# Counts of edges in windows of 16 nodes instead of 32, one incidence tile on ScalarE, and another order on VectorE and GpSimd

## What is computed

```python
h = maximum(_ln(x), 0)
m = mlp3(concat(h[src], h[dst], edge_attr), mW1, mW2, mW3)      # 32768 x 320 -> 256 -> 256 -> 128
summed = segment_sum(m, src) + segment_sum(m, dst)
x = x + mlp3(concat(h, summed, attention(h)), uW1, uW2, uW3)
h = maximum(_ln(x), 0)
deg = segment_sum(1, dst) + 1                                    # with a loop at every node
xw = h @ W
out = segment_sum(deg[src]**-.5 * deg[dst]**-.5 * xw[src], dst)  # loops included
x = x + gelu(out + b)
```

## Time and profile before

| | us |
|---|---|
| median of three runs | 767.0 |
| profiled execution, its own time | 765.72 |
| its span, first to last instruction | 763.9 |
| PE, DVE, ACT, POOL busy | 736.0, 729.5, 524.3, 539.0 |
| TensorE's mean granted clock | 0.994 |

### The profile page before, as it was taken

One profiled execution on the slowest core, in us unless ns is written; L12 is line 12 of the kernel. 1 busy time (PEld: TensorE's weight loads), 2 busy tenths in 40 slices (PEclk: granted clock), 3 DMA queues, 4 the chain that ended last, 5 costly groups with the idle time before them and its releaser, 6 DMA issues.

```text
span 763.9 us, 13342 instructions
## 1 busy us (share of the span) xinstructions
PE 736.0 (96%) x4171; PEld 619.3 (81%) x4171; DVE 729.5 (96%) x1506; ACT 524.3 (69%) x711; POOL 539.0 (71%) x533
## 2 busy tenths in 40 slices
PE   7589999999999999999999999999999999999896
PEld 6467888888888888888888888888888888888755
DVE  7889999999999999999999999999999999999775
ACT  3256777777777777777777777777777777776623
POOL 3777777777777777777777777777777777777100
PEclk9899999999999999999999999999999999999999
DMA  7534444344434444344443444434443444432000
GB/s 227 164 119 129 128 127 123 117 126 129 126 112 125 130 128 127 114 124 128 127 124 113 130 129 126 126 112 127 129 126 113 126 127 130 126 111 83 0 1 28
DMA packets 42566, 90.15 MB, mean 118 GB/s; under 512 B 11136, under 2 KB 17920, under 8 KB 42496
## 3 DMA queue, kind: packets, MB, share of 16 engines
q0 software_dynamic: 24576, 67.14, 28.6%
q1 hardware_dynamic: 17920, 22.16, 9.9%
HBM read 86.64 MB, written 2.62 MB: 117 GB/s over the span
## 4 chain that ended last, share of the span: by engine, by line
PE 88%; DVE 4%; POOL 3%; issue 2%; DMA 2%; ACT 1%; DVEq 0%; SPq 0%; POOLq 0%
PE bank L628 30%; PE bank L607 22%; PE bank L617 14%; PE bank L587 7%; PE bank L593 7%; PE bank L646 4%; POOL rows_sb L446 2%; POOL rows_sb L454 1%; DVE ring L1005 1%; PE bank L720 1%; DMA w_sb<-mW 1%; PE bank L765 1%; PE bank L728 1%; DMA table_a<-rows_sb 0%; PE bank L714 0%
## 5 line engine op out<-in xcount | busy, mean ns | idle before, releaser
L446 POOL DMA_INDIRECT rows_sb<-table_a,ends_i x256 | 263.5, 1029 | 82.2 <-issue 77.7
L454 POOL DMA_INDIRECT rows_sb<-table_b,ends_i x256 | 262.7, 1026 | 78.0 <-issue 78.0
L812 ACT ACTIVATE dist<-iota_h,neg_mid 128x1026 f16<-128x1026 f16 (+1 forms) x256 | 292.3, 1143 | 0.0
L1005 DVE TENSOR_SCALAR ring<-dist,half_gap,times 128x1026 fp32r<-128x1026 f16 (+1 forms) x256 | 276.4, 1081 | 1.7 <-ACT dist L812 0.6
L628 PE MATMUL bank<-ring,m_hi 128*128 128x512 f32 x512 | 172.4, 418 | 1.3 <-DVE ring L1005 1.1
L802 ACT ACTIVATE h_sb<-bank,b_sb 128x512 f32<-128x512 f32 x128 | 87.6, 684 | 122.5 <-PE bank L607 122.5
L628 PE MATMUL bank<-ring,m_lo 128*128 128x512 f32 x512 | 160.8, 395 | 0.0
L607 PE MATMUL bank<-ring,w_hi 128*128 128x512 f32 x512 | 150.0, 394 | 1.4 <-DVE ring L985 1.4
L1057 DVE TENSOR_SCALAR oh_key<-iota_h,key_f,minus_base 128x258 bf16<-128x258 f16 x321 | 128.5, 400 | 0.0
L617 PE MATMUL bank<-w_sb,h_sb 128*128 128x128 f32 x1024 | 124.8, 275 | 0.0
L593 PE MATMUL bank<-ident,rows_sb 128*128 128x128 f32 x512 | 113.7, 276 | 8.0 <-DVE rows_sb L1048 8.0
(11 more groups left out here) (182 smaller groups left out, 628.5 us busy)
## 6 DMA issues: line engine op xcount, KB each, us to landing
e_raw<-edge_attr_t SPq DMA_DIRECT2D x128, 128.0 KB, 3.1
rows_sb<-table_a,ends_i POOLq DMA_INDIRECT x256, 2.8
rows_sb<-table_b,ends_i POOLq DMA_INDIRECT x256, 2.9
table_a<-rows_sb SPq DMA_DIRECT2D x4, 256.0 KB, 3.4
table_b<-rows_sb SPq DMA_DIRECT2D x4, 256.0 KB, 2.5
x_sb<-x SPq DMA_DIRECT2D x2, 256.0 KB, 3.2
out<-oh_key SPq DMA_DIRECT2D x4, 128.0 KB, 1.8
u_sb<-uW SPq DMA_DIRECT2D x1, 384.0 KB, 5.0
```

Source lines behind the costliest of these rows:

```text
L446: nc.gpsimd.indirect_dma_start(got[:, b, t, 0, :], None, table_a, bass.IndirectOffsetOnAxis(ap=ends_i[:, 0, tile:tile + 1], axis=0),).then ...
L454: nc.gpsimd.indirect_dma_start(got[:, b, t, 1, :], None, table_b, bass.IndirectOffsetOnAxis(ap=ends_i[:, 1, tile:tile + 1], axis=0),).then ...
L812: nc.scalar.activation(to, of, ACT.Abs, bias=neg_mid[:, bass.ds(g * GT + t, 1)]).then_inc(dist_ready, 1)
L1005: nc.vector.tensor_scalar(to, of, half_gap[:, tile], times[:, tile], ALU.is_equal, ALU.mult).then_inc(inc_ready, 1)
```

## The change

The counts are made in 64 windows of 16 nodes, six tiles each, one window a group; `oh_key` is flat with 128 columns. The first six windows are made two at a time in DVE's groups -1, 0 and 1 and counted in PE's groups 0, 1 and 2. A pair of windows goes from PSUM to the counts by an add on DVE. `ct_sb` is cleared and its diagonal set at the start, on ACT, and `more_windows` runs then. Three incidence tiles stay on DVE, now all in rows, and the fourth is made on ACT as relu(times - times * abs(distance - gap)), except in the last group. DVE's list is reordered. In the last group the bias comes before the scatters, and the scatters go half by half. POOL only gathers.

The diff, cut to what matters:

```diff
-    VT = 10
-    NW = 32
+    VT = 6
+    NW = 64
     WD = N // NW
     WK = WD * NC
-    KR, KN, KP = 3, 86, 88
+    PAIRS = NW // 2
+    PD = 2 * WD
+    PK = 2 * WK
     MORE = NW * TILES
...
+    HOT = 4
     PAIR_ATT = 32
     DR, DN, DP = 3, 342, 344
-    IN_ROWS = (0, 2)
+    IN_ROWS = (0, 1, 2)
+    DT = GT - 1
     assert D == P and 2 * ED == P and H == 2 * P and GROUPS % 2 == 0
...
         ct_sb = sb("ct_sb", [P, NC, N])
         into_part = sb("into_part", [P, N])
-        from_part = sb("from_part", [P, NW, NC])
...
         w1_hi, w1_lo = inc[:, 1, 0:2 * H], inc[:, 1, 2 * H:4 * H]
-        iota_f = ct_sb[:, 0, :]
...
-        LAST_W = 2 * (NW - 1)
-
-        def made_in(i):
-
-            return 0 <= i and i + 1 < NW
-
-        def summed_in(b, i):
-
...
+        FILL = 2
+
+        def made_in(g):
+
+            if g < FILL:
+                return [2 * (g + 1), 2 * (g + 1) + 1]
+            return [w for w in (g + 2 + FILL,) if w < NW]
+
+        def counted_in(g):
+
+            if 0 <= g <= FILL:
+                return [2 * g, 2 * g + 1]
+            return [w for w in (g + 1 + FILL,) if FILL < g and w < NW]
+
+        def summed_in(g):
+
+            pairs = [p for p in range(PAIRS) if 2 * p + 1 in counted_in(g - 1)]
+            return pairs[0] if pairs else None
+
+        LAST_SUM = NW - 1 - FILL
...
-            pool.wait_ge(ld_w, 16 * 12)
-            nc.gpsimd.tensor_tensor(xb_sb[:, :, :], x_sb[:, :, :],
-                                    ub3_all[:, :].unsqueeze(1).broadcast_to([P, NC, D]), ALU.add).then_inc(xb_ready, 1)
-
-            pool.wait_ge(into_ready, 1)
-            diagonal = ct_all[:, 0:(NC - 1) * (N + P)].rearrange("p (s n) -> p s n", n=N + P)[:, :, 0:P]
-            nc.gpsimd.tensor_tensor(diagonal, diagonal, ident[:, :].unsqueeze(1).broadcast_to([P, NC - 1, P]), ALU.add)
-            diagonal = ct_all[:, (NC - 1) * (N + P):NC * N]
-            nc.gpsimd.tensor_tensor(diagonal, diagonal, ident[:, :], ALU.add).then_inc(self_added, 1)
-
...
                                           start=False, stop=True, is_transpose=True, skip_group_check=True)
-                    if counting and t in COUNTS_AT[k]:
...
+            def wait_incidence(g, t):
+
+                if t < DT or g == GROUPS - 1:
+                    pe.wait_ge(inc_ready, DT * g + (t + 1))
+                else:
+                    pe.wait_ge(last_inc_ready, g + 1)
+
...
-                if j % (VT // 2) == 0:
-                    pe.wait_ge(w_hot, 2 * w + j // (VT // 2) + 1)
-                if j == 0:
-                    wait(pe, w_out, w)
-                mm = nc.tensor.matmul(bank[2][:, 0:KR * KN], oh_low[:, w % HOT, j, :], oh_key[:, w % HOT, j, :, 0:KN],
-                                      start=(j == 0), stop=(j == VT - 1), skip_group_check=True)
-                if j == VT - 1:
-                    mm.then_inc(w_psum, 1)
+            def count_window(w):
+
+                pe.wait_ge(w_hot, w + 1)
+                if w % 2 == 0:
+                    wait(pe, w_out, w // 2)
+                at = (w // 2) % 2 * PK + w % 2 * WK
+                for j in range(VT):
+                    mm = nc.tensor.matmul(bank[2][:, at:at + WK], oh_low[:, w % HOT, j, :], oh_key[:, w % HOT, j, :],
+                                          start=(j == 0), stop=(j == VT - 1), skip_group_check=True)
+                mm.then_inc(w_psum, 1)
...
             def more_windows():
-                pe.wait_ge(w_out, NW)
                 visits = pe.value_load(rows_i[0:1, 2 * NW - 1:2 * NW], min_val=1, max_val=MORE)
                 with pe.Fori(0, visits) as v:
                     pe.wait_ge(more_hot, v + 1)
-                    nc.tensor.matmul(bank[2][:, 0:KR * KN], oh_low[:, 0, 0, :], oh_key[:, 0, 0, :, 0:KN],
+                    nc.tensor.matmul(bank[2][:, 0:WK], oh_low[:, 0, 0, :], oh_key[:, 0, 0, :],
                                      start=True, stop=True, skip_group_check=True).then_inc(more_psum, 1)
             def count_ends():
...
-                    mm = nc.tensor.matmul(acc_bank[c // 4][:, (c % 4) * P:(c % 4 + 1) * P], cb3[:, c, :], ident[:, :],
-                                          start=False, stop=(c % 4 == 3), is_transpose=True, skip_group_check=True)
-                    if c % 4 == 3:
-                        mm.then_inc(sums_ready, 1)
+                    nc.tensor.matmul(acc_bank[c // 4][:, (c % 4) * P:(c % 4 + 1) * P], cb3[:, c, :], ident[:, :],
+                                     start=False, stop=False, is_transpose=True, skip_group_check=True)
+
+            def last_scatter(g, b):
+
+                pe.wait_ge(m_lo_ready, g + 1)
+                for n in range(NH):
+                    for t in range(GT):
+                        if n == 0:
+                            wait_incidence(g, t)
+                        for part in (m_hi, m_lo):
+                            mm = nc.tensor.matmul(acc_bank[n][:, :], part[:, b, t, :], inc[:, t, n * HB:(n + 1) * HB],
+                                                  start=False, stop=(t == GT - 1 and part is m_lo),
+                                                  skip_group_check=True)
+                    mm.then_inc(sums_ready, 1)
...
+                if g == GROUPS:
+                    add_bias_of_sums()
+                    last_scatter(g - 1, 1 - b)
+                    return
...
                 if nxt:
-                    first_layer(g + 1, 1 - b, i + b, 0, counts_of(g))
+                    first_layer(g + 1, 1 - b, i + b, 0)
                 if past:
                     scatter(g - 1, 1 - b, 0)
                 if nxt:
-                    first_layer(g + 1, 1 - b, i + b, 1, counts_of(g))
+                    first_layer(g + 1, 1 - b, i + b, 1)
+                for w in counted_in(g):
+                    count_window(w)
                 if now:
                     messages(g)
-                if g == LAST_W + 1:
+                if g == LAST_SUM + 1:
...
             pe.wait_ge(w_lo_ready, 4)
+            pe.wait_ge(rows_ready, 1)
+            more_windows()
             pe.wait_ge(w1e_lo_ready, 1)
-
-            pe.wait_ge(rows_ready, 1)
             run_groups(pe, group, FIRST + 1)
...
+            def clear_counts(chunks):
+
+                for c in chunks:
+                    nc.scalar.activation(ct_sb[:, c, :], iota_h[:, 0:N], ACT.Copy, scale=0.0).then_inc(ct_zero, 1)
+
+            act.wait_ge(dve_step, 2)
+            clear_counts(range(0, NC - 2))
...
-                wait(act, inc_ready, GT * g + (t - 3))
+                if t < DT:
+                    wait(act, inc_ready, DT * (g - 1) + t + 1)
+                else:
+                    wait(act, last_inc_ready, g)
                 to, of = dist[:, t, 0:N], iota_h[:, 0:N]
-                if t in IN_ROWS:
+                if t in IN_ROWS and g < GROUPS - 1:
                     to = dist[:, t, :].rearrange("p (r n) -> p r n", r=DR)[:, :, 0:DN]
                     of = iota_h[:, :].rearrange("p (r n) -> p r n", r=DR)
                 nc.scalar.activation(to, of, ACT.Abs,
                                      bias=neg_mid[:, bass.ds(g * GT + t, 1)]).then_inc(dist_ready, 1)
+            def last_gap(g):
+
+                act.wait_ge(dist_ready, GT * g + GT)
+                nc.scalar.activation(dist[:, DT, 0:N], dist[:, DT, 0:N], ACT.Abs,
+                                     bias=neg_gap[:, bass.ds(g * GT + DT, 1)]).then_inc(gap_ready, 1)
+
+            def last_incidence(g):
+
+                act.wait_ge(gap_ready, g + 1)
+
+                wait(act, scattered, GT * g)
+                tile = bass.ds(g * GT + DT, 1)
+                nc.scalar.activation(inc[:, DT, 0:N], dist[:, DT, 0:N], ACT.Relu, bias=times[:, tile],
+                                     scale=neg_times[:, tile]).then_inc(last_inc_ready, 1)
...
+                if past:
+                    distance(g - 1, 2)
                 if now:
                     relu_second(g, 0)
                 if past:
-                    distance(g - 1, 2)
+                    distance(g - 1, 3)
                 if now:
                     relu_second(g, 1)
+                if past and now:
+                    last_gap(g - 1)
                 if nxt:
                     relu_first(g + 1, 1 - b, 0)
-                if past:
-                    distance(g - 1, 3)
+                if past and now:
+                    last_incidence(g - 1)
...
-                if summed_in(b, i):
-                    window_out(i)
-
-            def window_out(w):
-
-                act.wait_ge(w_psum, w + 1)
-                nc.scalar.copy(ct_sb[:, :, bass.ds(w * WD, WD)],
-                               bank[2][:, 0:WK].rearrange("p (d a) -> p a d", a=NC)).then_inc(w_out, 1)
...
+            clear_counts(range(NC - 2, NC))
+            act.wait_ge(ct_zero, NC)
+            act.wait_ge(consts_pool, 7)
+            diagonal = ct_all[:, 0:(NC - 1) * (N + P)].rearrange("p (s n) -> p s n", n=N + P)[:, :, 0:P]
```

(98 more changed lines are left out.)

70 lines of the change are left out of this document (26 added, 44 removed).

## The result

The changed kernel takes **782.1 us** (median of four runs, 780.3 to 783.5) against 766.9: ratio **1.020**, interval 1.017 to 1.023. Forecast were 762 and "faster"; it is 2% slower, outside the range of 754 to 771. The profiled execution took 783.08 us, its span 781.3.

A forecast was written before the change was run, and what follows sets the result against it. PE sets the pace, with DVE 1% behind. Start +8.6, loop -8.7, groups 61 and 62 -0.7, `count_ends` +1.7, end -5.8: -4.9 us off the median 767.0 gives 762, range 754 to 771.

The forecast's parts named there:

- PE's work: PE per group: five count matmuls (0.54 us) become six of 0.06 (0.36), so the group falls from 10.67 to 10.49.
- weight-bound: Rival, `count_window` on PE: 0.104 us a matmul as with one column, group 10.75, 777 us; chance 0.08.
- half-cheap counts: Rival, PE's counts: spacing 0.08 us, midway between the two bounds, 767 us; chance 0.12.
- the second `add_pair` of the next group but one ends 8.9 us after that first start: DVE's list from `low_first`, 5.5 us after PE's second layer: ends at 14.45 in a group with sums; PE wants 14.4.
- That is a stall of some 0.06 every second group: PE's wait for DVE's second `add_pair` in the loop; group taken as 10.52, 58 groups save 8.7 us.
- DVE and ACT pace the loop: Rival, loop: chain from the ReLU to `add_pair` 0.15 us longer, groups 10.65, 769 us; chance 0.20.
- This is 0.34 under PE: DVE per group: busy 10.6 us before, 10.15 after the change, against PE's 10.49.
- sets nothing: POOL's gathers: 1.25 us each, 10.0 a group, with 10.5 a group left and three buffers of lead.
- The second `add_pair` of group 3 ends at 74.4: Start, DVE pacing the fill: group 0 ends at 58.2 us, group 1 at 71.9, then this add at 74.4.
- the same without bias: Start, DVE's group 1: group 0's terms less bias, plus two incidences, pair 1.2, passes 0.6; ends at 71.9 us.
- PE does the rest of that group: Start, PE in group 3: scatter 1.0, transposes 0.6, counts 0.7, messages 1.7, scatters 2.9, to 81.3 us.
- The end: Group 63's second layer to the update's first matmul: 13.9 us for 19.6, 5.8 less.

The follow-up runs named there:

- e13: Changed kernel with 0.0 in place of the pointer to the window's base in `oh_key`, still two operations: 770.3 us, ratio 1.006.
- e14: Changed kernel with `oh_key` as one operation with one pointer, the window's base left out: 770.5 us, ratio 1.004.
- the order run: Changed kernel with ACT's `last_incidence` behind both `relu_first` instead of between them: 778.1 us, ratio 1.015.
- e15: Changed kernel with the rows form of `oh_key`, two rows of 64 instead of flat: 781.0 us, ratio 1.019.
- sums later: Changed kernel with `pair_sums` one group after `pair_out` instead of in the same group: 781.9 us, ratio 1.021.
- e1: Changed kernel with incidence tile 1 flat again, so two tiles in rows instead of three: 773.5 us, ratio 1.009.
- new operation: Three-rows kernel with all helpful edits; one `tensor_scalar` over 128x6 a window adds the base, so `oh_key` has one pointer: 766.2 us, ratio 0.9996.
- e18: Last edit: two-rows kernel with all helpful edits and the base added by one operation, first one-hots moved back ahead of the first add: 759.6 us, ratio 0.991.
- Fill 1: Changed kernel with windows made two at a time in groups -1 and 0 only, not in 1: 776.2 us, ratio 1.013.
- busy PE: Changed kernel with 22 and 9 unused matmuls on PE before the first layer in groups 1 and 2: 779.8 us, ratio 1.017.
- the run with the change's end alone: Kernel before, with bias transposes first, the last scatter in halves and group 63's incidence flat: 766.0 us, ratio 0.998.

## Why the prediction was wrong, point by point

- **PE's work: right.** Count matmuls 0.055 for 0.06, the group 10.51 for 10.49. The rivals of weight-bound and half-cheap counts are out. So are the Trainium skill's 81 ns (TensorE: Matmul & The Clock Gate, Back-to-back issue gap) for a sustained stream: this trace disagrees, with 55 ns in runs of six bf16 matmuls of 128 columns.
- **The loop failed at "the second `add_pair` of the next group but one ends 8.9 us after that first start" and "That is a stall of some 0.06 every second group".** The list takes 9.45 and the stall is 0.55. The mechanism was the named rival (DVE and ACT pace the loop), its size mis-judged too: it had the chain 0.15 longer, it is 0.55 longer. Two terms: `oh_key` "taken like `oh_low` at 0.17" is 0.22 for its second pointer, five in the list (e13, e14: -0.29); the second `low_first` waits 0.20 for ACT's `last_incidence` (the order run: -0.21). I took 7.05 for that ReLU's end and 5.5 for `low_first`'s start, both right within 0.05, but let the rest of the list start from the 5.5. The chain explains the slow groups of all runs in which neither a gather nor DVE's whole work is the bound:

| edit | chain | slow group |
|---|---|---|
| none, rows form of the key, sums later | 11.06 | 11.06, 11.05, 11.08 |
| tile 1 flat (e1) | -0.52 = 10.54 | none, 10.51 as PE's own |
| ACT's order | -0.20 = 10.86 | 10.85 |
| one pointer (e13, e14) | -0.28 = 10.78 | 10.76, 10.77 |
| ACT's order, one pointer, new operation | 10.71 | 10.72 |

- **DVE's margin.** "This is 0.34 under PE" compared means, and was 0.2 (10.56 for 10.15; the six keys are 0.3 of it). It couldn't have settled the matter: every second group has `pair_sums` in the chain, 0.86, and DVE can't work ahead since `low_first` waits for PE's first layer. The prediction saw that and went by the chain; what failed are the chain's prices. Its margin, under 0.1, was less than either term that it missed.
- **POOL "sets nothing": right for the changed kernel** (sums-later run; DVE never waits for a gather), wrong once the chain is shortened by a flat incidence: gathers then set the pace at 10.6 to 10.95, until the order of the last run. The flat tile isn't all of it: with ACT's order alone they came at 11.0.
- **The start: group 0 right (43.1 for 42.7), the fill wrong by 7.** "The second `add_pair` of group 3 ends at 74.4" came at 79.0: batches 0.3 to 0.4 longer each, and waits of DVE for ACT of 1.16 in group 0 and 1.07 and 0.48 in group 1, where I had 0.9 and none (the terms "the same without bias" add up to 72.8 with the waits; the 71.9 leaves them out). `count_passes` took 1.1 for 0.6, and a pair of one-hots of group 2 stood ahead of its add, 0.4. "PE does the rest of that group" "to 81.3", 6.9 us, took 9.4: PE's granted clock was 0.50 from 60.3 to 67.0 and from 77.4 to 84.1, behind its waits, which the prediction had only for the first group. Fill 1 (-5.8 at group 5) and busy PE (-3.4) bear out the two parts; the second gain is near the spread of the start.
- **The end: right** (-5.5 for -5.8; 14.2 us to the update's first matmul for 13.9), though in part for another reason than I gave: the order of the last matmuls brings nothing, so, less the 1.1 of the run with the change's end alone, it is by elimination mostly the visit that left the end.

Shown are the chain, its two terms, the cost of the double batch in group 1, the clock behind PE's waits, and that DVE's order changes the gathers' pace. Open are what the clock was worth in the whole time, and why nearly the same DVE work gives gathers at 10.5 or at 11.0 a group.

## What to carry to other kernels

Where work alternates, cost the heavier period along its chain, not the mean of each engine's sum: PE was bound by a list on another engine though that engine had 0.2 us a group to spare on average. Then compare the margin with what the prices can be off: here five operations priced by a similar one with one pointer less, and one wait behind another engine's tile, made 0.55 of a stall of 0.06. When such a list is shortened, look for the next bound: here one pair of one-hots on the wrong side of an add decided 18 us through another engine's DMA issues. And a fill that makes PE wait costs the wait and the clock after it.

## What the hardware showed that was not expected

- A per-partition pointer as second scalar costs 0.06 us on a 128x128 `tensor_scalar` (0.22 with two pointers, 0.16 with one, one or two operations alike; e13, e14).
- Flat or in two rows of 64, the same operation takes 0.22 (e15); on 1024 elements the flat incidence took 0.73 and the one in rows 1.25.
- After waits of 4.28 and 1.16 us, and again of 1.88 and 1.16, PE's granted clock was 0.56 over 6.8 us (much of it at 1.2 of its 2.4 GHz); with matmuls in the waits it was 1.00.
- A gather is held by adds and by one-hots or flat operations next to them: 318.54 + 1.34 beside an add to 318.98, 413.22 + 1.80 beside add and one-hots to 414.10, against 0.95 alone; in both it ends 0.9 after them. In the changed kernel all 109 gathers that took over 1.0 between 101 and 690 ran beside an add (80) or beside `low_edges` (29), both with two inputs in SBUF, and ended 0.8 to 0.9 after it; of those that began beside `low_first`, `low_messages` or `pair_sums` none took over 1.0.
- The Trainium skill (SBUF — State Buffer, Who interferes with whom) infers that operations with two SBUF inputs don't block descriptor writing; the add, which has two, holds the gather here as in the earlier trace rows. The same section lets such operations contend with GpSimd operations that read SBUF. These gathers do, as their indices `ends_i` lie there; no run tells whether that is the reason.
- Gathers have no fixed rate: from 10.49 (e18) to 11.0 us a group (the ACT run) with the same 512, by what stands beside them on DVE and when.
